# Expert up projection with the weights as stationary operand, copied per tile to two fixed buffers

## The reference, cut to what matters

```python
xf = x.reshape(b * n, d)                      # 4096 tokens x 256
logits = xf @ gate_w + gate_b
one_hot = jax.nn.one_hot(jnp.argmax(logits, axis=-1), E)      # E = 8
h = jax.nn.gelu(jnp.einsum('td,edh->teh', xf, w1), approximate=True)   # hidden width 1024
y = jnp.einsum('teh,ehd->ted', h, w2)
out = jnp.einsum('te,ted->td', one_hot, y)
...
x = _layernorm(x + ffn(x))                    # over the last axis
```

## Time and profile before

| what | value |
|---|---|
| median of 3 runs | 1610.31 us |
| the profiled execution's own time | 1609.57 us |
| its span | 1607.7 us |
| PE busy | 1367.2 us (85%) |
| ACT busy | 960.1 us (60%) |
| DVE busy | 819.5 us (51%) |
| POOL busy | 330.8 us (21%) |
| `down` (line 658), PE busy | 141.8 us in 624 instructions |
| `up` (line 637), PE busy | 142.4 us in 312 instructions |
| mean granted TensorE clock | 0.945 of 2.4 GHz |

### The profile page before, as it was taken

The page is one execution under the profiler, slowest core; times in us unless marked ns, Lnnn a source line. Parts: engine busy times, 40 slices in busy tenths (PEclk is TensorE's granted clock), DMA queues, the critical chain, the costliest instruction groups (busy, mean ns, idle before and its releaser), DMA issues. The chain is left out here.

```text
span 1607.7 us, 25085 instructions
## 1 busy us (share of the span) xinstructions
PE 1367.2 (85%) x6614; PEld 639.2 (40%) x6615; DVE 819.5 (51%) x1950; ACT 960.1 (60%) x1809; POOL 330.8 (21%) x337
## 2 busy tenths in 40 slices
PE   3499898898898889899979996999983599999993
PEld 1233333343333333343424342434332366666662
DVE  3233463553543368777757775777841333333331
ACT  0267776876776656666646664666660266666663
POOL 4122231332232111122212221222121111111110
PEclk9699999999999999999989998999995699999997
DMA  6211312313213212122212221212246211111113
GB/s 159 91 49 64 125 53 82 118 37 103 98 43 121 93 40 96 38 80 65 69 56 80 61 73 56 80 54 80 94 144 235 72 49 49 49 49 49 49 49 124
DMA packets 109626, 127.77 MB, mean 79 GB/s; under 512 B 8304, under 2 KB 102128, under 8 KB 109392
## 3 DMA queue, kind: packets, MB, share of 16 engines
q1 hardware_dynamic: 77696, 79.46, 15.7%
q10 hardware_dynamic: 27392, 33.56, 6.4%
q0 software_dynamic: 4432, 13.52, 2.7%
HBM read 51.51 MB, written 28.46 MB: 50 GB/s over the span
## 5 line engine op out<-in xcount | busy, mean ns | idle before, releaser
L695 ACT ACTIVATE w_space<-bank 128x512 f32<-128x512 f32 x1024 | 569.7, 600 | 320.9 <-PE bank L458 303.4
L458 PE MATMUL bank<-w_space 96*128 96x512 bf16 (+1 forms) x1024 | 367.5, 388 | 58.4 <-ACT w_space L695 23.2
L882 DVE TENSOR_REDUCE negm<-bank 128x1 f32<-128x512 f32 x512 | 327.5, 684 | 119.3 <-PE bank L485 115.5
L472 PE MATMUL bank<-w_space 128*32 128x512 f32 x2048 | 282.8, 625 | 13.6 <-ACT w_space L695 10.8
L485 PE MATMUL bank<-w_space 96*128 96x512 bf16 x512 | 198.5, 388 | 30.1 <-ACT neg_T L708 13.2
L458 PEld LDWEIGHTS bank<-w_space 96*128 96x128 bf16 (+1 forms) x1024 | 99.1, 100 | 256.3 <-ACT w_space L695 136.7
L658 PE MATMUL bank<-w_space,work_space 128*128 x624 | 141.8, 380 | 1.6 <-DVE work_space L1162 1.6
L637 PE MATMUL bank<-w_space,work_space 128*128 x312 | 142.4, 600 | 0.6 <-DVE work_space L1153 0.6
L485 PEld LDWEIGHTS bank<-w_space 96*128 96x128 bf16 x512 | 49.5, 97 | 214.0 <-DVE negm L882 98.3
L523 PE MATMUL bank<-work_space,wqkv_sb 128*128 128x512 f32 x256 | 125.2, 612 | 5.6 <-DVE w_space L1002 4.8
L658 PEld LDWEIGHTS bank<-w_space,work_space 128*128 128x128 f32 x624 | 115.6, 190 | 16.4 <-issue 2.3
(11 more groups left out here) (134 smaller groups left out, 1608.3 us busy)
## 6 DMA issues: line engine op xcount, KB each, us to landing
w_space<-work_space SPq DMA_DIRECT2D x384, 128.0 KB
w_space<-in_w_dram ACTq DMA_DIRECT2D x16, 1024.0 KB, 7.6
work_space<-in_x_dram ACTq DMA_DIRECT2D x16, 512.0 KB
work_space<-rows_dram SPq DMA_DIRECT2D x39, 128.5 KB, 2.1
work_space<-rows_dram SPq DMA_DIRECT2D x39, 128.0 KB, 2.1
x_dram<-xo SPq DMA_DIRECT2D x32, 128.0 KB, 1.7
h_dram<-row_sb SPq DMA_DIRECT2D x32, 128.0 KB, 3.0
work_space<-h_dram ACTq DMA_DIRECT2D x8, 512.0 KB
```

Of the source, the lines that this page charges most:

```text
L458: nc.tensor.matmul(L.st_banks[c % n][:, :], k_stack[0:L.rows, s, h, kt * P:(kt + 1) * P], q_stack[0:L.rows, s, h, :], start=True, stop=Tru ...
L472: last = nc.tensor.matmul(L.pv_banks[g % n][VW * j:VW * (j + 1), :], v_aug[:, s, kt, HEADS_AT_ONCE * g + j, :], probs[:, q % 2, j, :], sta ...
L695: nc.scalar.activation(probs[:, q % 2, j, :], L.st_banks[c % len(L.st_banks)][:, :], ACT.Exp, scale=SCALE).then_inc(L.exps, 1)
L882: ve.tensor_reduce(negm[:, c % TT, c // TT:c // TT + 1], L.mx_ring.bank(use)[:, :], axis=AX.X, op=ALU.max, negate=True).then_inc(L.mx_ring ...
```

## The change

In the new kernel `w1` is the stationary operand of `up` and `xsT` moves, 128 columns at a time: 8 pieces of the hidden width, two matmuls each. The result has the hidden width on the partitions, as `down` needs it; ACT writes it straight to `hidT`. `transpose_hidden` on PE and `hidden` on DVE are gone. `up` uses four banks (2s + n), and waits for the GELU of tile j-2 only.

The stationary operand is read from two fixed buffers. DVE copies a tile's whole `w1` there (`weights_of`): it loads the expert's number, waits for `up(j-2)`, and copies 128 x 2048 fp32. In DVE's list `weights_of(j+1)` stands between `tile_in(j+1)` and `tile_out(j-2)`. The buffers are `w1_first` in the work space and `w1_late` in the space of the attention weights. PE now loads the expert's number once per body, at the head of `down`, behind `transpose_in`. DVE waits for all of `w1` before its first copy, PE for all of `w2`.

```diff
--- before.py
+++ after.py
@@ -265,11 +265,15 @@
         rs = rs[:, 0, :]
         (w1_sb,) = carve(w1_space, [("e k f", dict(e=E, k=KD, f=F), FP32)])
         (w2_sb,) = carve(w2_space, [("e k d", dict(e=E, k=KF, d=D), FP32)])
-        xs_sb, xsT, hid, hidT, rest_sb, z_sb, o_sb, by_tile = carve(work_space, [
+        (w1_late,) = carve(wqkv_sb[:, :, :, :].rearrange("p a k n -> p (a k n)"), [
+            ("k f", dict(k=KD, f=F), FP32)])
+        w1_first, xs_sb, xsT, hidT, rest_sb, z_sb, o_sb, by_tile = carve(work_space, [
+            ("k f", dict(k=KD, f=F), FP32),
             ("s d", dict(s=2, d=D), FP32), ("s k t", dict(s=2, k=KD, t=P), FP32),
-            ("s f", dict(s=2, f=F), FP32), ("s k t", dict(s=2, k=KF, t=P), FP32),
+            ("s k t", dict(s=2, k=KF, t=P), FP32),
             ("s d", dict(s=2, d=ROW - D), FP32), ("s d", dict(s=2, d=D), FP32),
             ("s d", dict(s=2, d=D), FP32), ("n t e", dict(n=3, t=TILES, e=E), FP32)])
+        w1_tile = (w1_first, w1_late)
         past, began, row_at = (by_tile[0:1, n, :, :] for n in range(3))
 
 
@@ -315,10 +319,9 @@
         rest_in = [sem("rest_in0"), sem("rest_in1")]
         xs_T = sem("xs_T")
         xsT_ready = sem("xsT_ready")
+        w1_ready = sem("w1_ready")
         up_done = sem("up_done")
         gelu_done = sem("gelu_done")
-        hid_T = sem("hid_T")
-        hidT_ready = sem("hidT_ready")
         down_done = sem("down_done")
         sum_done = sem("sum_done")
         last_stats = sem("last_stats")
@@ -615,11 +618,7 @@
             pipeline(pe, body)
 
             pe.wait_ge(tiles_ready, 1)
-            for arrived in weights_in:
-                pe.wait_ge(arrived, 16 * E)
-
-            def expert_of(j):
-                return pe.value_load(tile_expert[0:1, bass.ds(j, 1)], min_val=0, max_val=E - 1)
+            pe.wait_ge(weights_in[1], 16 * E)
 
             def transpose_in(j, s):
                 pe.wait_ge(xs_in[s], 8 * (j - s) + 16)
@@ -629,30 +628,23 @@
                                                xs_sb[:, s, k * P:(k + 1) * P], ident_sb[:, :])
                 last.then_inc(xs_T, 1)
 
-            def up(j, s, e):
+            def up(j, s):
                 pe.wait_ge(xsT_ready, j + 1)
+                pe.wait_ge(w1_ready, j + 1)
                 for n in range(2):
-                    wait(pe, gelu_done, 2 * j + (n - 1))
-                    for k in range(KD):
-                        last = nc.tensor.matmul(
-                            psum[n][:, :], xsT[:, s, k, :],
-                            w1_sb[:, bass.ds(e, 1), k, n * T:(n + 1) * T].rearrange(
-                                "p a f -> p (a f)"),
-                            start=(k == 0), stop=(k == KD - 1))
+                    wait(pe, gelu_done, 2 * j + (n - 3))
+                    for f in range(KF // 2):
+                        at = (n * KF // 2 + f) * P
+                        for k in range(KD):
+                            last = nc.tensor.matmul(
+                                psum[2 * s + n][:, f * P:(f + 1) * P],
+                                w1_tile[s][:, k, at:at + P],
+                                xsT[:, s, k, :], start=(k == 0), stop=(k == KD - 1))
                     last.then_inc(up_done, 1)
 
-            def transpose_hidden(j, s):
-                for n in range(2):
-                    pe.wait_ge(gelu_done, 2 * j + (n + 1))
-                    wait(pe, hidT_ready, 2 * j + (n - 1))
-                    for k in range(KF // 2):
-                        at = n * T + k * P
-                        last = nc.tensor.transpose(psum[2 + n][:, k * P:(k + 1) * P],
-                                                   hid[:, s, at:at + P], ident_sb[:, :])
-                    last.then_inc(hid_T, 1)
-
-            def down(j, s, e):
-                pe.wait_ge(hidT_ready, 2 * j + 2)
+            def down(j, s):
+                e = pe.value_load(tile_expert[0:1, bass.ds(j, 1)], min_val=0, max_val=E - 1)
+                pe.wait_ge(gelu_done, 2 * j + 2)
                 wait(pe, sum_done, j)
                 for k in range(KF):
                     last = nc.tensor.matmul(
@@ -662,15 +654,13 @@
                 last.then_inc(down_done, 1)
 
             def expert_body(j, s, ends=False):
-                this, last = expert_of(j), expert_of(j - 1)
-                transpose_hidden(j - 1, 1 - s)
-                up(j, s, this)
+                up(j, s)
                 if not ends:
                     transpose_in(j + 1, 1 - s)
-                down(j - 1, 1 - s, last)
+                down(j - 1, 1 - s)
 
             transpose_in(0, 0)
-            up(0, 0, expert_of(0))
+            up(0, 0)
             transpose_in(1, 1)
             expert_body(1, 1)
             expert_body(2, 0)
@@ -679,8 +669,7 @@
                 expert_body(2 * pair + 2, 0)
             expert_body(TILES - 2, 1)
             expert_body(TILES - 1, 0, ends=True)
-            transpose_hidden(TILES - 1, 0)
-            down(TILES - 1, 0, expert_of(TILES - 1))
+            down(TILES - 1, 0)
 
 
         @block.scalar
@@ -837,8 +826,10 @@
                 for n in range(2):
                     act.wait_ge(up_done, 2 * j + (n + 1))
                     if n == 0:
-                        wait(act, hid_T, 2 * j - 2)
-                    nc.scalar.activation(hid[:, s, n * T:(n + 1) * T], psum[n][:, :],
+                        wait(act, down_done, j - 1)
+                    half = hidT[:, s, n * KF // 2:(n + 1) * KF // 2, :]
+                    nc.scalar.activation(half.rearrange("p k t -> p (k t)"),
+                                         psum[2 * s + n][:, :],
                                          ACT.Gelu_apprx_tanh).then_inc(gelu_done, 1)
 
             def last_norm(j, s):
@@ -1153,14 +1144,12 @@
                 ve.tensor_copy(xsT[:, s, :, :].rearrange("p k t -> p (k t)"), psum[4][:, 0:D]
                                ).then_inc(xsT_ready, 1)
 
-            def hidden(j, s):
-                for n in range(2):
-                    dve.wait_ge(hid_T, 2 * j + (n + 1))
-                    if n == 0:
-                        wait(dve, down_done, j - 1)
-                    half = hidT[:, s, n * KF // 2:(n + 1) * KF // 2, :]
-                    ve.tensor_copy(half.rearrange("p k t -> p (k t)"), psum[2 + n][:, :]
-                                   ).then_inc(hidT_ready, 1)
+            def weights_of(j, s):
+                e = dve.value_load(tile_expert[0:1, bass.ds(j, 1)], min_val=0, max_val=E - 1)
+                wait(dve, up_done, 2 * j - 2)
+                ve.tensor_copy(w1_tile[s][:, :, :].rearrange("p k f -> p (k f)"),
+                               w1_sb[:, bass.ds(e, 1), :, :].rearrange("p a k f -> p (a k f)")
+                               ).then_inc(w1_ready, 1)
 
             def tile_sum(j, s):
 
@@ -1183,14 +1172,18 @@
                                  ALU.subtract, ALU.mult).then_inc(out_ready, 1)
 
             def expert_body(j, s, first=False, ends=False):
-                hidden(j - 1, 1 - s)
                 if not ends:
                     tile_in(j + 1, 1 - s)
+                    weights_of(j + 1, 1 - s)
                 if not first:
                     tile_out(j - 2, s)
                 tile_sum(j - 1, 1 - s)
 
+            dve.wait_ge(tiles_ready, 2)
+            dve.wait_ge(weights_in[0], 16 * E)
+            weights_of(0, 0)
             tile_in(0, 0)
+            weights_of(1, 1)
             tile_in(1, 1)
             expert_body(1, 1, first=True)
             for j in range(2, 5):
@@ -1200,7 +1193,6 @@
                 expert_body(2 * pair + 2, 0)
             expert_body(TILES - 2, 1)
             expert_body(TILES - 1, 0, ends=True)
-            hidden(TILES - 1, 0)
             tile_out(TILES - 2, 1)
             tile_sum(TILES - 1, 0)
             tile_out(TILES - 1, 0)
```

## The result

The change makes the kernel slower: 1665.02 us at the median (1664.42 to 1665.86, 4 runs) against 1611.03 us (1609.34 to 1615.49, 4 runs), a ratio of 1.034 with a 95% interval of 1.0312 to 1.0368. The forecast was 1668 us. The profiled execution took 1665.86 us, its span is 1663.8 us: 56.1 us more than the span before.

A forecast was written before the change was run, and what follows sets the result against it. PE (7.99 us per tile) and a loop through DVE, POOL, scatter, SP and input load (7.97) bind together; 35 x (9.81 - 8.07) = +60.7, -2.45 and -0.5 turn 1609.57 into 1667.3, stated as 1668 us, range 1646 to 1700.

The forecast's parts named there:

- The main step: On DVE, `weights_of` delays `tile_out` to 2.14 us after `tile_in` instead of 0.34, lengthening each tile's loop; chance 0.78.
- the loop: `tile_in`, `tile_out`, POOL's scatter, SP's `load_rest` and `load_tile`, back to `tile_in`: 7.97 us per tile, growing to 9.81.
- `up` on PE: 32 matmuls of 128 columns with weight loads hidden take 3.5 us; 7.0 us if loads and streams add up.
- PE alone would neither gain nor lose: PE's new tile is 8.0 us: the transposes' 0.87 us are spent again, 0.6 on the register load, the rest on overheads.
- The ends: Outside the steady state: -0.5 us at the start (bodies 1 and 2), -2.45 us at the last tile's `down`.
- The clock: PE's waiting may halve its clock; one low stretch per tile costs 1.7 us of matmul work, in the forecast at no cost.
- The open weight loads: Rival in `up` on PE: loads don't hide, `up` 7.0 us, PE's tile 11.5 us, time 1727 us; chance 0.09.
- the slow copy: Rival on DVE: the copy runs at PSUM's slope, 2.25 instead of 1.2 us, loop 10.86, time 1705 us; chance 0.06.
- the slack in the landing: Rival at SP: the scatter's landing sets the pace, `tile_out`'s delay misses the input load; 1605 us, faster or equal 0.03.
- the clock alone: Rival on PE: two low stretches per tile make it 11.4 us, some 1723; something between, 1690 to 1720; chance 0.04.

The follow-up runs named there:

- useless copy in the old kernel: Kernel before, with DVE also loading the number and copying `w1` to an unread buffer between `tile_in` and `tile_out`: 1662.42 us against 1606.86, ratio 1.034.
- half copy: Changed kernel with only the first 1024 of 2048 elements per partition of `w1` copied: 1648.38 us against 1606.86 before, ratio 1.026.
- number load moved ahead: Changed kernel with DVE's load of the expert's number ahead of `tile_in`, the copy left in place: 1647.31 us against 1614.24 before, ratio 1.020.
- inputs-ahead kernels: Changed kernel with SP loading tile j+2's inputs ahead of tile j's rest: 1580.64 us; with PE's number load also moved to the head of `up`: 1574.95 us.

## Why the prediction was right, and where it was not

**The main step held, for the reason given.** The forecast had the loop grow by 1.80 us to 9.81; it grew by 1.74 in `tile_out`'s delay (2.08 instead of 2.14) and the tiles follow at 9.75. The terms: register load to the copy's start 0.94 (I took 1.0), copy 1.23 (1.2). As written, 1.0 + 1.2 - 0.08 is 2.12 and not 2.14, which is worth 0.7 us in the sum; and the chances of the forecast add up to 1.02. The useless copy in the old kernel shows that the copy and its register load alone make this time. The half copy and the number load moved ahead show that it goes by the amount, and the inputs-ahead kernels show that it goes through the input load: there the delay stays and the time is gone.

**`up` on PE** took 3.57 us for 32 instructions; I had 3.5. The loads hide under streams of 128 columns. The figure of the Trainium skill for pairs of a weight load and a matmul of 128 columns (TensorE: Matmul & The Clock Gate, "Back-to-back issue gap"), which my estimate scaled to 0.16 us, can't be carried over to these fp32 pairs in that way: 0.112 us each was measured.

**"PE alone would neither gain nor lose" was wrong.** The step that failed is the 0.95 us from the weight load of `transpose_in` to that of `down`. I took the register load there as always in the open. It is so only when the inputs come late or just in time, since PE's sequencer runs ahead of its matmuls until an instruction has to wait (register load at 1404.6, end of `up` at 1406.40, in the inputs-ahead kernel). In that kernel PE's tile is 7.25 us, not 8.0; in the changed kernel, where the inputs are late, it is 0.44 + 0.61 + 3.46 + 3.57 = 8.08 us without the wait, as I had it. The change thus carries a gain of 7.98 - 7.25 = 0.73 us per tile: the 0.87 us of transposes, less 0.13 for `up` (3.57 against 3.44). The loop hides it. This did not hurt the number, since the loop was the longer one in any case, but it hid what the change is worth.

**The ends were mis-sized, and cancel in part.** At the start I had -0.5 us and -1.9 was measured, but half of that is not the change's: DVE's last instruction ahead of the experts starts at 1259.33 us in the profiled execution before and at 1258.29 in the one after, 1.0 us earlier, which is variation. The first `tile_in` comes another 0.5 us sooner, for a reason that no run isolates. From there to the `tile_in` of tile 3 it takes 18.8 us instead of 19.2, so 0.4 was won in the tiles, near the forecast. At the end I had -2.45 and it was -0.5. The last `down` waited 0.71 us, where I had it wait for nothing, for the residual sum of the tile before: both use one bank, and the transposes no longer stand between them.

```profile
1633.43 3.62 PE L650 MATMUL bank<-w_space,work_space 128*128 x16
1637.76 3.72 PE L650 MATMUL bank<-w_space,work_space 128*128 x16 [0.71 <-DVE work_space L1158]
```

And one `down` in this stretch ran at the low clock (5.40 us from 1624.62), 1.9 us longer. The smaller terms, which I left out, come to -0.7: the last transposes of a hidden layer -0.9, the register load +0.5, `up` +0.1, the stretch behind the last `down` -0.4. The sum of the two ends is -2.4 us against -2.95 in the forecast, and that they come so close is luck: 1.0 of it is variation, and the low clock happened to fall on this `down`. The rest of the difference between 1667.3 and 1665.86 us is the loop, 35 x 0.06 = 2 us less.

**The clock** fell in 9 of 35 tiles, once in each, where the forecast allowed one low stretch per tile at no cost. It cost almost nothing in the steady state, since PE had time to spare: with the 1.9 us more for `down` PE came as late as the loop. In five tiles it was a little later, 9.80 to 9.84 us where the others of the same half of the loop body take about 9.6, some 1 us in all.

**The rivals.** The open weight loads, the slow copy and the slack in the landing are all refuted by the rows of the changed kernel. That the clock alone could make it 1690 to 1720 us did not come about: there was never more than one low stretch in a tile.

## What to carry to other kernels

A chain of waits that runs through one busy engine doesn't show what is almost as long. Before work is put on another engine, follow the instructions that stand behind the place in that engine's list, through queues and DMAs, until they come back to where they began; here a loop within 0.02 us of PE's time could be read from start times, and what was put into it came out almost in full (1.74 us in, 1.67 out). If such a loop is in the way, the remedy may be the order of a queue's list: letting the input load wait for the scatter of one tile earlier turned a loss of 3.4% into a gain of 2.2%.

## What the runs showed of the hardware that was not expected

- DVE's copy within SBUF stretches a scatter instruction that POOL issues at the same time from 0.96 to 1.59 us. Placed behind `tile_sum` it costs the scatter nothing (0.96 us).
- A register load on PE behind an instruction that waits is exposed (0.61 us to the next matmul). Where the wait was over in time it costs nothing: it began 1.8 us before the matmuls ahead of it had ended.
- With fp32 weight loads of 128 columns for every 128 columns streamed PE keeps one matmul instruction per 0.112 us (32 in 3.57 us), nearly the 0.109 us of the transposes.
